# Squared lengths of the delta queries: one square and matmuls with a column of ones, in place of eight turns and eight squares

## The reference, cut to what matters

```
qkv = silu(causal_conv1d(x @ W_qkvz))            # q, k: 16 heads x 128; v: 32 heads x 128
q = q * rsqrt(sum(q * q, -1) + 1e-6) * 128**-0.5 # per token and head
k = k * rsqrt(sum(k * k, -1) + 1e-6)
...                                              # chunks, triangular solve, recurrence over a state
core = rmsnorm(core * silu(z)) * norm_weight     # mean over the 128 value channels, eps 1e-6
out = core @ W_out
```

## Time and profile before

| | us |
|---|---|
| median of 3 executions | 2116.94 |
| lowest and highest | 2115.31, 2123.66 |
| the profiled execution | 2107.43 |
| its span | 2105.7 |
| tensor engine busy in the span | 1625.7 (77%) |
| VectorE busy | 1182.7 (56%) |
| ScalarE busy | 896.2 (43%) |
| GpSimd busy | 594.8 (28%) |

### The profile page before, as it was taken

The page is one execution under the profiler, slowest core; times in us unless marked ns, Lnnn a source line. Parts: engine busy times, 40 slices in busy tenths (PEclk is TensorE's granted clock), DMA queues, the critical chain, the costliest instruction groups (busy, mean ns, idle before and its releaser), DMA issues. The chain is left out here.

```text
span 2105.7 us, 43832 instructions
## 1 busy us (share of the span) xinstructions
PE 1625.7 (77%) x16605; PEld 1172.4 (56%) x16605; DVE 1182.7 (56%) x2521; ACT 896.2 (43%) x2414; POOL 594.8 (28%) x981
## 2 busy tenths in 40 slices
PE   5878950086013699999999999999999999866998
PEld 2433430064001477777777777777777777754555
DVE  5774158033334566676677667766765776443444
ACT  2226810022002456556555655666566656331111
POOL 5001005601720332442343245224523432320000
PEclk9999965588555899999999999999999999887999
DMA  4000001086342211211121122212211210101111
GB/s 135 1 2 2 1 4 71 26 256 206 103 40 59 44 22 26 50 35 33 35 50 27 26 51 40 37 26 51 46 27 30 50 31 8 25 1 31 37 37 42
DMA packets 174671, 95.91 MB, mean 46 GB/s; under 512 B 100933, under 2 KB 165054, under 8 KB 174480
## 3 DMA queue, kind: packets, MB, share of 16 engines
q1 hardware_dynamic: 162768, 75.47, 14.8%
q0 software_dynamic: 6144, 13.12, 2.8%
q10 hardware_dynamic: 5568, 4.72, 0.7%
HBM read 71.46 MB, written 25.36 MB: 46 GB/s over the span
## 5 line engine op out<-in xcount | busy, mean ns | idle before, releaser
L1597 DVE SCALAR_TENSOR_TENSOR d_conv<-d_big,d_cw,d_conv 128x1023 f32<-128x1023 f32 (+2 forms) x192 | 245.3, 1278 | 42.2 <-ACT d_conv L1758 39.4
L1356 PE MATMUL d_big<-all_xn_t,d_w 128*128 128x512 f32 x512 | 247.7, 613 | 26.9 <-DMA d_w<-in_L_attn_W_qkvz 15.1
L1938 POOL TENSOR_TENSOR d_y<-d_y,all_xn 128x256 f32<-128x256 f32 x128 | 94.8, 741 | 262.3 <-DVE d_y L1729 220.9
L1356 PEld LDWEIGHTS d_big<-all_xn_t,d_w 128*128 128x128 f32 x512 | 95.4, 197 | 106.0 <-issue 89.8
L1894 POOL TENSOR_TENSOR d_sv<-d_ek,d_half 128x8 f32<-128x8 f32 x16 | 26.2, 1637 | 427.3 <-DVE d_ek L1623 398.4
L1569 PE MATMUL d_big<-d_wo,d_yt 128*128 128x256 f32 x512 | 145.0, 440 | 0.9 <-ACT d_yt L1876 0.9
L2100 PE MATMUL e_gu<-all_xn_t,e_up_w 128*128 128x512 f32 x272 | 121.4, 600 | 15.1 <-DMA e_dn_w<-in_L_ffn_Wd 15.1
L1758 ACT ACTIVATE d_conv<-d_big,d_cw 128x1024 f32<-128x1024 f32 x64 | 71.4, 1116 | 132.2 <-issue 78.0
L1569 PEld LDWEIGHTS d_big<-d_wo,d_yt 128*128 128x128 f32 x512 | 111.4, 226 | 19.9 <-issue 1.2
L1861 ACT COPY d_ys<-d_big 128x128 f32<-128x128 f32 x256 | 60.4, 268 | 142.8 <-PE d_big L1525 123.6
L147 PE MATMUL ln_turned<-all_ident,all_xn 128*128 128x128 f32 x64 | 17.5, 441 | 132.7 <-DVE all_xn L127 132.7
(11 more groups left out here) (321 smaller groups left out, 3953.6 us busy)
## 6 DMA issues: line engine op xcount, KB each, us to landing
d_w<-in_L_attn_W_qkvz SPq DMA_DIRECT2D x16, 768.0 KB
e_gu<-in_L_ffn_gate_up_proj SPq DMA_DIRECT2D x48, 192.0 KB, 3.3
d_G<-decay_rows_scratch SPq DMA_DIRECT2D x32, 256.0 KB, 6.2
slots_scratch<-l_zero SPq DMA_DIRECT2D x1, 4608.0 KB
e_xe<-slots_scratch SPq DMA_DIRECT2D x48, 96.0 KB, 3.2
e_dn<-in_L_ffn_down_proj SPq DMA_DIRECT2D x48, 96.0 KB, 3.6
expert_out_scratch<-e_ye ACTq DMA_DIRECT2D x48, 96.0 KB, 3.4
d_E<-decay_rows_scratch SPq DMA_DIRECT2D x16, 256.0 KB, 7.9
```

The costliest lines, as they stand in the source:

```text
L1356: mm = pe.matmul(big[0][:, c, :], w_sb[par][:, k, n * DK:(n + 1) * DK], xn_t[:, k, c * 512:(c + 1) * 512], start=(k == 0), stop=(k == KD - 1))
L1597: dve.scalar_tensor_tensor(conv[:, sh:T], src[:, 0:T - sh], cw[:, bass.ds(g, 1), COLUMN_OF[j], 3 - sh], conv[:, sh:T], ALU.mult, ALU.add). ...
L1938: pool.tensor_tensor(part, part, zs[:, t, :], ALU.mult).then_inc(s["yg_s"], 1)
```

## The change

The eight transposes of q and the eight squares of its token rows are removed. ScalarE squares q as it lies, 128 channels by 1024 tokens, in one instruction into a new buffer `q_sq`. The tensor engine then does eight matmuls, one for each tile of 128 tokens: the squares are the stationary operand (128 channels by 128 tokens), a column of ones is the moving one, and the result is one column of bank 6 with a sum for each token. VectorE reads the 8 columns straight from PSUM for `qe`.

The steps move. `qnorm` stands where `qturn` stood on the tensor engine. `qsq` stands on ScalarE between `tap0 2` and `ksq 2`, ahead of this group's `l2p`; the two old steps stood after `ys 0` and `ys 1`. `qe` on VectorE moves from the following iteration to the place right before `products 0` of its own group, behind `tap 2 3`. `products 0` waits for `qe`, and `products 1` for nothing of its own.

```diff
-    kturn, proj 2 0; this l1y; next proj 2 1; this l2p 0, l2p 1, l2y 0, l2y 1; next qturn; this y 0, kv 0, iv 0, ks 1, y
+    kturn, proj 2 0; this l1y; next proj 2 1; this l2p 0, l2p 1, l2y 0, l2y 1; next qnorm; this y 0, kv 0, iv 0, ks 1, y
...
-    this l0p; next tap 1 1, tap 1 2; this qe; next tap 1 3; this l0x; ...
-    l1y, l2p; next tap 2 1; this l2y; next tap 2 2, kb; this state 0, gather 0, r 1; next tap 2 3, products 0; this
+    this l0p; next tap 1 1, tap 1 2, tap 1 3; this l0x; ...
+    next tap 2 1; this l2y; next tap 2 2, kb; this state 0, gather 0, r 1; next tap 2 3, qe, products 0; this state 1;
...
-    tap0 2, ksq 2; this l2p; next ksq 3; this l2y, ys 0; next qsq 0; this ys 1; next qsq 1; this o1 1, sq2 0; next silu
+    tap0 2, qsq, ksq 2; this l2p; next ksq 3; this l2y, ys 0, ys 1, o1 1, sq2 0; next silu 2; ...
...
-            def qturn(g, par):
+            def qnorm(g, par):
                 pe.wait_ge(s["kc_s"], g + 1)
-                pe.wait_ge(s["silu_s"], g * NJ + 2)
-                eight(lambda t: kq[par][:, 1, t * P:(t + 1) * P]).then_inc(s["qt_t"], 1)
+                pe.wait_ge(s["qq_s"], g + 1)
+                for t in range(TT):
+                    mm = pe.matmul(bank[6][:, t:t + 1], q_sq[:, t * P:(t + 1) * P], ones[:, :], start=True, stop=True,
+                                   skip_group_check=True)
+                mm.then_inc(s["qn_mm"], 1)
 
             def products(g, par, i):
-                if i < 2:
-                    pe.wait_ge(s["sq_s"], g * 16 + 12 + 4 * i)
-                else:
+                if i == 0:
+                    pe.wait_ge(s["qe_s"], g + 1)
+                elif i > 1:
                     pe.wait_ge(s["ai_s"], g * 4 + i - 1)
...
             def qe_(g, par):
-                dve.wait_ge(s["sq_s"], g * 16 + 16)
+                dve.wait_ge(s["qn_mm"], g + 1)
                 if not at(g, 0) and not at(g, 1):
                     dve.wait_ge(s["rn2_e"], g * 4 - 4)
-                dve.tensor_scalar(qe[par][:, :], ss[:, 1, :], EPS, EPS * DK, ALU.add, ALU.mult).then_inc(s["qe_s"], 1)
+                dve.tensor_scalar(qe[par][:, :], bank[6][:, 0:TT], EPS, EPS * DK, ALU.add, ALU.mult).then_inc(s["qe_s"], 1)
...
-            def qsq(g, par, i):
-                if i == 0:
-                    act.wait_ge(s["qt_t"], g + 1)
-                    if not at(g, 0):
-                        act.wait_ge(s["qe_s"], g)
-                for t in range(4 * i, 4 * i + 4):
-                    act.activation(junk[:, :], bank[6 + t // 4][:, (t % 4) * P:(t % 4 + 1) * P], ACT.Square,
-                                   accum_out=ss[:, 1, t:t + 1]).then_inc(s["sq_s"], 1)
-                    act.wait_ge(s["sq_s"], g * 16 + 8 + t + 1)
+            def qsq(g, par):
+                act.wait_ge(s["silu_s"], g * NJ + 2)
+                if not at(g, 0):
+                    act.wait_ge(s["qn_mm"], g)
+                act.activation(q_sq[:, :], kq[par][:, 1, :], ACT.Square).then_inc(s["qq_s"], 1)
```

More of the change, by code:

```diff
@@ L1141 @@
     prev state 6, r 7, gather 6; this vturn 1; next shift 0, tap 0 1, tap 0 2, tap 0 3, shift 1; prev gather 7, yn 1;
-    this l0p; next tap 1 1, tap 1 2; this qe; next tap 1 3; this l0x; prev out_mm 1 0, out_mm 1 1; next cross; this l1p,
-    l1y, l2p; next tap 2 1; this l2y; next tap 2 2, kb; this state 0, gather 0, r 1; next tap 2 3, products 0; this
-    state 1; next products 1; this r 2; next products 2; this state 2, gather 1, r 3; next products 3; this gather 2,
-    gather 3, state 3, r 4; next vturn 0; this state 4, gather 4, r 5, yn 0, state 5; next tap 3 1; this r 6; next tap 3
-    2, tap 3 3; this gather 5, out_mm 0 0, out_mm 0 1
+    this l0p; next tap 1 1, tap 1 2, tap 1 3; this l0x; prev out_mm 1 0, out_mm 1 1; next cross; this l1p, l1y, l2p;
+    next tap 2 1; this l2y; next tap 2 2, kb; this state 0, gather 0, r 1; next tap 2 3, qe, products 0; this state 1;
+    next products 1; this r 2; next products 2; this state 2, gather 1, r 3; next products 3; this gather 2, gather 3,
+    state 3, r 4; next vturn 0; this state 4, gather 4, r 5, yn 0, state 5; next tap 3 1; this r 6; next tap 3 2, tap 3
+    3; this gather 5, out_mm 0 0, out_mm 0 1
 """)
@@ L1151 @@
     3; next tap0 1, decay; prev out_turn 1; this l0y; next silu 1; this l1p; next kturn, ksq 0, ksq 1; this l1y; next
-    tap0 2, ksq 2; this l2p; next ksq 3; this l2y, ys 0; next qsq 0; this ys 1; next qsq 1; this o1 1, sq2 0; next silu
-    2; this o1 2, ys 2, ys 3, o1 3, sq2 1, sq2 2, sq2 3, ys 4, o1 4; next tap0 3; this o1 5, ys 5, out_turn 0, ys 6, o1
-    6; next silu 3; this sq2 4
+    tap0 2, qsq, ksq 2; this l2p; next ksq 3; this l2y, ys 0, ys 1, o1 1, sq2 0; next silu 2; this o1 2, ys 2, ys 3, o1
+    3, sq2 1, sq2 2, sq2 3, ys 4, o1 4; next tap0 3; this o1 5, ys 5, out_turn 0, ys 6, o1 6; next silu 3; this sq2 4
 """)
@@ L1180, in delta1_phase @@
         vs = [m.sb(f"vs{i}", [P, GR, TT, DK]) for i in range(2)]
-        ss = m.sb("ss", [P, 2, TT])
+        ss = m.sb("ss", [P, TT])
+        q_sq = m.sb("q_sq", [P, T])
         ek = m.sb("ek", [P, TT])
@@ L1220, in delta1_phase @@
         w_in = [m.sem(f"w_in{i}") for i in range(2)]
-        names = ("setup const_s rows_in wo_in proj_mm tap_s conv_v silu_s kt_t kc_s qt_t sq_s ek_s sv_s bk_s qe_s x_s exp_s edge_s "
+        names = ("setup const_s rows_in wo_in proj_mm tap_s conv_v silu_s kt_t kc_s qq_s qn_mm sq_s ek_s sv_s bk_s qe_s x_s exp_s edge_s "
                  "kk_mm ai_s blk_out blk_in sol_v sol_s sol_out y_in vt_t vs_s kout_s p0_mm p0_s y0_mm x0_mm y0_s x0_s p1_mm p1_s "
@@ L1571, in out_mm @@
                 mm.then_inc(s["out_mm"], 1)
-            loop(pe, PE_ORDER, dict(proj=proj, kturn=kturn, qturn=qturn, products=products, vturn=vturn, l0p=l0p, l0y=l0y, l0x=l0x,
+            loop(pe, PE_ORDER, dict(proj=proj, kturn=kturn, qnorm=qnorm, products=products, vturn=vturn, l0p=l0p, l0y=l0y, l0x=l0x,
                                     l1p=l1p, l1y=l1y, l2p=l2p, l2y=l2y, gates=gates, ks=ks, qs=qs, y=solve_y, kv=kv, iv=iv,
@@ L1620, in kb @@
             def kb(g, par):
-                dve.wait_ge(s["sq_s"], g * 16 + 8)
-                dve.tensor_scalar(ek[:, :], ss[:, 0, :], EPS, None, ALU.add).then_inc(s["ek_s"], 1)
+                dve.wait_ge(s["sq_s"], g * 8 + 8)
+                dve.tensor_scalar(ek[:, :], ss[:, :], EPS, None, ALU.add).then_inc(s["ek_s"], 1)
                 dve.wait_ge(s["ek_s"], g + 1)
@@ L1781, in ksq @@
                 for t in (2 * i, 2 * i + 1):
-                    act.activation(junk[:, :], k_tok[:, t, :], ACT.Square, accum_out=ss[:, 0, t:t + 1]).then_inc(s["sq_s"], 1)
-                    act.wait_ge(s["sq_s"], g * 16 + t + 1)
-            def qsq(g, par, i):
-                if i == 0:
-                    act.wait_ge(s["qt_t"], g + 1)
-                    if not at(g, 0):
-                        act.wait_ge(s["qe_s"], g)
-                for t in range(4 * i, 4 * i + 4):
-                    act.activation(junk[:, :], bank[6 + t // 4][:, (t % 4) * P:(t % 4 + 1) * P], ACT.Square,
-                                   accum_out=ss[:, 1, t:t + 1]).then_inc(s["sq_s"], 1)
-                    act.wait_ge(s["sq_s"], g * 16 + 8 + t + 1)
+                    act.activation(junk[:, :], k_tok[:, t, :], ACT.Square, accum_out=ss[:, t:t + 1]).then_inc(s["sq_s"], 1)
+                    act.wait_ge(s["sq_s"], g * 8 + t + 1)
+            def qsq(g, par):
[3 more added lines that the diff above has]
+                act.activation(q_sq[:, :], kq[par][:, 1, :], ACT.Square).then_inc(s["qq_s"], 1)
             def decay(g, par):
```

## The result

The changed kernel takes 2206.89 us (median of 4, 2204.24 to 2214.95), the kernel before 2116.98 us: 4.25% slower, ratio 1.0425, 95% interval 1.039 to 1.046. The forecast was 2157 with a range of 2126 to 2190: the sign was right, the size (40 us) less than half of the 90 that came.

The account below looks back on a forecast made before the run. The tensor engine was taken to bound the kernel. Over 15 groups, 0.80 (matmuls) + 0.75 and 1.05 (waits), plus 1.2 us at the start, made 40.2 us on 2116.9: 2157 us, range 2126 to 2190.

Parts of the forecast that it names:

- The view of the bound: Whole kernel: the tensor engine bounds, busy 1625.7 of 2105.7 us; ScalarE's savings count only where the tensor engine waits for it.
- The noise floor: Groups of equal instructions: one to three microseconds a group hang on when the clock falls.
- Part 1: `qnorm` on the tensor engine: 16 records 0.108 us apart, 1.73 us in place of 0.93, +0.80 us a group.
- The step that failed: Stretch around `qnorm`: taken to stay at full clock, as all of 1183 to 1202 did; nothing added to the sum.
- the clock falls in the changed stretch: Rival: `qnorm` itself runs at half clock, 1.73 us more a group, 26 us, 2183 us in all; chance 0.15.
- Parts 2 and 4: Tensor engine waits: 0.75 us a group in `l2y` for ScalarE's copy, 1.05 before `products 0` for VectorE's `qe`.
- Parts 3 and 5: Squares of q taken off ScalarE: worth 0 on the path; later steps: no slack grows to take the delay up.
- The stretch before the first iteration: Group 0's steps running alone: `products 0` starts 1.7 us later; taken as +1.2 us, bounds 0 and 1.9.

Follow-up runs that it names:

- b_square: Kernel before plus one ScalarE square of q over 128x1024 ahead of `l2p`, into a buffer that nobody reads: 2144.5 us, ratio 1.0119.

## Why the prediction was wrong

**The view of the bound** held. The tensor engine ends the stage, and what ScalarE gained (28 us of busy time) came to nothing. The noise floor was put too low: the rows that the prediction cites, 68.3 to 74.3 us for equal groups, lie up to 6 us apart, and not one to three.

**Where the time of a group went**, by starts on the tensor engine, as means over the 15 groups of the two profiled executions:

| from, to | before | after | more | forecast |
|---|---|---|---|---|
| first to last record of `l2y` (the square's wait) | 1.83 | 2.64 | 0.81 | 0.75 |
| last record of `l2y` to `y 0` (`qnorm` for the turns) | 1.08 | 3.45 | 2.37 | 0.80 |
| `y 0` to `y 1` | 2.80 | 4.12 | 1.32 | 0 |
| `y 1` to `products 0` (the wait for `qe`) | 0.58 | 1.61 | 1.03 | 1.05 |
| `products 0` to `kv 1` | 0.87 | 1.27 | 0.40 | 0 |
| the rest of the group | 65.33 | 65.68 | 0.35 | 0 |

Both waits were met almost exactly, though a little of each is records that ran slow (in the group read above they are 0.69 and 0.94). What was missing is in `qnorm` and in the unchanged steps behind it.

**Part 1, the spacing of the records**, held at full clock: 0.112 us against 0.108. That it isn't the moving columns that price them is shown by the run with 128 of them, 0.118 us. That it is the load of 32-bit floats fits, but is argued: loads of the same 128x128 in bfloat16 stood 0.025 us apart. The Trainium skill's table of 25 ns for up to 64 columns ("TensorE: Matmul & The Clock Gate", section "Back-to-back issue gap") agrees with the bfloat16 run (0.025 us) and not with 32-bit floats. The term itself, 12 us, measured 1.19% or 25 us by the run with 128 columns and no waits. In the group read above, `y 0` starts 1.89 us after `qnorm`'s first record, against 0.93 in the earlier trace rows: 0.96 us, so 14 us are seen in the step. The other 11 us or so lie behind `kv 1`, 0.80 us a group, where the late stretch of half clock was longer in that run's profile (6.6 us a group against 5.5). Whether that follows from the edit stays open.

**The step that failed** is the one by which the changed stretch stays at full clock. I had it as a rival, "the clock falls in the changed stretch", with a chance of 0.15 and a price of 26 us, and left it out of the sum because 1183 to 1202 ran at 1.00. It falls in all 15 groups. Two things were wrong with it. The chance: I took the calm of the stretch as a property of the stretch, when it rested on the eight transposes that the edit removed (8.9 us a group with the one-column records, 1.8 with transposes) and on there being no wait ahead of them (`b_square`). The rows to weigh were there: the router's short matmuls never left half clock, and the new step puts 16 of that kind straight behind the solve's small ones. And the price: I charged half clock for the new step alone, 1.73 us, while it lasts through `y 0`, `kv 0` and `iv 0`, 8.9 us a group. By the table above, `qnorm` took 1.41 us more than the 0.96 that its records cost at full clock, and the steps from `y 0` to `kv 1`, without the wait for `qe`, 1.72 more: an estimate of 3.1 us a group, 47 us, for a term that stood at 0 in the sum and at 26 in the rival.

**Parts 2 and 4, the two waits**, have the mechanism and the size: 0.81 for 0.75 and 1.03 for 1.05, 15 x 1.84 = 28 us. (As the profile counts idleness, they are 0.57 and 0.64. The first square of k began 0.95 us after the big square did, 1397.48 to 1398.43, not 1.06.) Taken away together they give back 2.1%, 44 us (1.0425 to 1.0216), and 1.9% with 128 columns (1.0306 to 1.0119). That is more than the waits themselves; with them part of the early half clock goes (8.9 to 4.1 us a group, and 3.0 to 0). Taken away singly they give 0.8% and 0.7%; the rest comes only when both are gone. That the shares do not add up is shown; how they combine is not.

**Parts 3 and 5** are borne out: the rest of the group did not get shorter, and the idle time before the line of L1436 went from 49.9 to 58.3 us (PE and PEld together), so nothing later took the delay up.

**The sum, as the runs split it:** 16 records for 8, 1.19% (forecast 12 us, got 25); one column and not 128, 0.97% (forecast 0, got 21); the waits with what they do to the clock, 2.1% (forecast 27, got 44). Together 4.25%, 90 us. The split depends on its order: with both waits in place one column and not 128 costs 1.19% (1.0425 against 1.0306).

**The stretch before the first iteration** took 83.8 us, 80.3 before: 3.5 where 1.2 was forecast; the other versions lay between 81.8 and 83.8. The kernel before with nothing but a square more (`b_square`) is one of them, with 82.8, so how much of the 3.5 is the edit's is open.

## What to carry to other kernels

When a tensor engine step is replaced, ask what it did for the clock. Behind the solve's small matmuls eight transposes, or 128 moving columns, with no wait before them left the clock at 2.4 GHz where one moving column did not, and the fall was paid mostly by what ran behind it; a wait of 0.57 us in the same place cost three times its length. The column of the granted clock, read over the step and the 10 us behind it, decides that at a glance. A reduction over partitions by a column of ones cost here two records 0.11 us apart for each tile in 32-bit floats and one record of 0.025 in bfloat16, so use it in bfloat16 where the sum may be that coarse (here it only enters a term times epsilon). Even so the gain over the turns was 0.2% at best, since what they had covered was then waited for.

## What the hardware showed that I had not expected

- Moving 128 columns of ones in place of one made the same sums in less time: 2141.8 against 2159.5 us, with the loads unchanged.
- A ScalarE instruction that nobody reads, 1.05 us in each group on an engine that is busy 43% of the time, cost 26 us (ratio 1.0119).
- One-column matmuls on bfloat16 squares stand 0.025 us apart, four and a half times closer than on 32-bit floats (0.112), and there are half as many records: 0.2 us in place of 1.8 for the same eight tiles.
